# Attention in a graph and transformer kernel: the fp32 product of probabilities and values replaced by three one-pass products

## The reference

```python
h = _layernorm(x, ln1_g, ln1_b)
q = (h @ wq + bq).reshape(B, S, N_HEADS, dk)      # the first block has no biases
k = (h @ wk + bk).reshape(B, S, N_HEADS, dk)
v = (h @ wv + bv).reshape(B, S, N_HEADS, dk)
scores = jnp.einsum('bqhd,bkhd->bhqk', q, k) / np.sqrt(dk).astype(np.float32)
attn = jax.nn.softmax(scores, axis=-1)
ctx = jnp.einsum('bhqk,bkhd->bqhd', attn, v).reshape(B, S, D)
x = x + ctx @ wo + bo
h2 = _layernorm(x, ln2_g, ln2_b)
moe_out = _moe(h2.reshape(-1, D), router_w, router_b, w1, b1, w2, b2)
return x + moe_out.reshape(B, S, D)
```

## Time and profile before

| what | value |
|---|---|
| time, median of 3 | 3896.92 us |
| profiled execution: its own time | 3900.6 us |
| its span | 3898.9 us |
| mean granted TensorE clock | 0.861 of full speed |
| TensorE matmul busy | 2943.6 us (75%) |
| VectorE busy | 1631.0 us (42%) |
| ScalarE busy | 808.3 us (21%) |
| GpSimd busy | 187.3 us (5%) |
| line 804, values product, x960 records | 376.9 us busy |
| line 955, maxima, x480 | 269.8 us busy |
| line 893, exponentials, x480 | 230.9 us busy |

### The profile page before, as it was taken

The page is one execution under the profiler, slowest core; times in us unless marked ns, Lnnn a source line. Parts: engine busy times, 40 slices in busy tenths (PEclk is TensorE's granted clock), DMA queues, the critical chain, the costliest instruction groups (busy, mean ns, idle before and its releaser), DMA issues. The chain is left out here.

```text
span 3898.9 us, 41895 instructions
## 1 busy us (share of the span) xinstructions
PE 2943.6 (75%) x12919; PEld 1988.3 (51%) x12920; DVE 1631.0 (42%) x3241; ACT 808.3 (21%) x1669; POOL 187.3 (5%) x215
## 2 busy tenths in 40 slices
PE   5888739976999972998578589965865688898735
PEld 3555516555666641665264266653643556665523
DVE  6777651134566532343523601030132346565323
ACT  1222310103444410111201211110111124443100
POOL 0000000000000003111100000001010000000033
PEclk9999869998999975998788799967977899999767
DMA  6000270200000005996420300005322000000054
GB/s 244 2 0 0 49 220 13 51 22 9 6 6 3 0 3 151 307 312 198 115 108 2 80 6 11 1 1 166 122 70 51 25 11 4 5 3 0 1 171 131
DMA packets 123973, 261.27 MB, mean 67 GB/s; under 512 B 40586, under 2 KB 41818, under 8 KB 122587
## 3 DMA queue, kind: packets, MB, share of 16 engines
q1 hardware_dynamic: 47643, 122.34, 10.3%
q10 hardware_dynamic: 46848, 92.38, 7.3%
q0 software_dynamic: 29376, 45.16, 4.0%
HBM read 185.71 MB, written 74.02 MB: 67 GB/s over the span
## 5 line engine op out<-in xcount | busy, mean ns | idle before, releaser
L804 PE MATMUL ps<-probs,V 125*128 125x500 f32 (+1 forms) x960 | 376.9, 514 | 0.0
L955 DVE TENSOR_REDUCE mx<-ps 125x1 f32<-125x500 f32 (+1 forms) x480 | 269.8, 588 | 170.0 <-PE ps L787 167.4
L893 ACT ACTIVATE probs<-ps 125x500 f32<-125x500 f32 (+1 forms) x480 | 230.9, 517 | 373.8 <-PE ps L796 363.4
L243 PE MATMUL ps<-onehot_src,onehot_dst 125*128 x1200 | 259.5, 356 | 42.3 <-DVE onehot_dst L219 16.1
L218 DVE TENSOR_SCALAR onehot_src<-iota,src_f 125x1250 f16 x400 | 218.2, 545 | 113.4 <-PE ps L243 100.7
L795 PE MATMUL ps<-Q_hi_twice,K_hi_lo 128*125 128x500 f32 (+1 forms) x480 | 208.7, 435 | 61.2 <-DVE Q_hi_twice L937 32.2
L787 PE MATMUL ps<-K_hi_lo,Q_hi_twice 128*125 128x500 f32 (+1 forms) x480 | 219.5, 464 | 16.0 <-DVE mx L955 7.3
L1377 PE MATMUL ps<-w2s,hT 128*78 128x512 f32 (+1 forms) x480 | 218.1, 601 | 3.6 <-ACT hT L1402 3.6
L804 PEld LDWEIGHTS ps<-probs,V 125*128 125x128 f32 x960 | 164.0, 192 | 105.9 <-issue 105.0
L1442 DVE COPY yb<-ps 78x512 f32<-78x512 f32 (+1 forms) x100 | 68.8, 688 | 348.4 <-PE ps L1377 270.3
L243 PEld LDWEIGHTS ps<-onehot_src,onehot_dst 125*128 x1200 | 121.7, 102 | 173.7 <-issue 118.7
(11 more groups left out here) (341 smaller groups left out, 4681.8 us busy)
## 6 DMA issues: line engine op xcount, KB each, us to landing
room<-in_L_ffn_w_p ACTq DMA_DIRECT2D x72, 512.0 KB, 5.6
w2s<-in_L_ffn_w ACTq DMA_DIRECT2D x72, 512.0 KB, 6.6
buf<-zeros SPq DMA_DIRECT2D x37, 512.0 KB
slabs<-ah_spill SPq DMA_DIRECT2D x20, 585.9 KB
xb<-buf SPq DMA_DIRECT2D x64, 156.0 KB
yb<-yb POOLq DMA_DIRECT2D x64, 156.0 KB, 6.6
xb<-buf SPq DMA_DIRECT2D x36, 250.0 KB
tv<-in_L_ffn_tv_W_p SPq DMA_DIRECT2D x2, 4096.0 KB
```

The source lines that it names most:

```text
L243: mm_ = pe.matmul(ps[:, 3 * half + c, 0:cn], ohd[:, slot, :].rearrange("p o n -> p (o n)"), ohs[:, slot, c0:c0 + cn].rearrange("p o n -> p ...
L804: mm = pe.matmul(ps[:, ACC + n, 0:cn], V[:, t, :], PT[:, t % 2, c0:c0 + cn], start=(t == 0), stop=(t == T - 1))
L893: act.activation(PT[:, t % 2, c0:c0 + cn], ps[0:P, ST + n, 0:cn], ACT.Exp, scale=SCALE).then_inc(p_out, 1)
L955: v.tensor_reduce(mx[:, t, n:n + 1], ps[0:P, SQ + cc % 2, 0:cn], AX.X, ALU.max)\
```

## The change

- The probabilities exist in two f32r halves. ScalarE writes each exponential twice, to PH (rounded to f32r) and to PT (fp32). GpSimd makes PL = PT - PH in one instruction of 125x1250 per tile.
- V is split into VH and VL the same way, once per head on VectorE.
- The values product is now VH PH + VL PH (times_v) and, two tiles later, VH PL (rest_times_v), behind a semaphore p_lo of GpSimd. lo_done counts it and frees the PL slot and, for the last tile, the context.
- minus_max uses f32r operands with an identity of 126 columns, and its third row lies in bank ST+2. The projection's third chunk and minus_max(0) wait accordingly.
- Tile 0 of a head waits chunk by chunk for the projection's copies and the row, no longer for all.
- PT, wo and bo now lie in the memory of x (`spare`). x is written to DRAM (x_spill) in the first norm block of the transformer and read back in the norm block behind attention.
- The constant tri is freed after the start.

```diff
+        VH, VL = pair("V", [P, T, 128])
+        PT = spare(P, (2, N))
+        PH, PL = pair("probs", [P, 2, N])
+        eye = sb("eye_r", [P, P + 1], f32r)
...
-        ROW = [ps[DH:DH + 1, SQ, 0:500], ps[DH:DH + 1, SQ + 1, 0:500], ps[0:1, SQ, 0:250]]
+        ROW = (SQ, SQ + 1, ST + 2)
...
                 def times_v(h, t, n):
                     c0, cn = CH[n]
-                    if n == 0:
-                        pe.wait_ge(p_out, h * 30 + (3 * t + 3))
-                    mm = pe.matmul(ps[:, ACC + n, 0:cn], V[:, t, :], PT[:, t % 2, c0:c0 + cn],
-                                   start=(t == 0), stop=(t == T - 1))
+                    pe.wait_ge(p_hi, h * 30 + (3 * t + n + 1))
+                    pe.matmul(ps[:, ACC + n, 0:cn], VH[:, t, :], PH[:, t % 2, c0:c0 + cn], start=(t == 0), stop=False)
+                    mm = pe.matmul(ps[:, ACC + n, 0:cn], VL[:, t, :], PH[:, t % 2, c0:c0 + cn], start=False,
+                                   stop=False)
...
+                def rest_times_v(h, t):
+                    pe.wait_ge(p_lo, h * T + (t + 3))
+                    for n, (c0, cn) in enumerate(CH):
+                        mm = pe.matmul(ps[:, ACC + n, 0:cn], VH[:, t, :], PL[:, t % 2, c0:c0 + cn], start=False,
+                                       stop=(t == T - 1))
+                    mm.then_inc(lo_done, 1)
...
-                            mm = pe.matmul(ROW[n][:, P * t - c0:P * t - c0 + P], negm[:, t:t + 1],
-                                           k.ident[0:P, 0:P], start=True, stop=True)
+                            o = (P + 1) * (t - c0 // P)
+                            mm = pe.matmul(ps[0:1, ROW[n], o:o + P + 1], negm[:, t:t + 1],
+                                           eye[:, :], start=True, stop=True, skip_group_check=True)
...
                 def tiles(h, j, those, has_next, has_second):
                     for t in those:
-                        if t == 0:
-                            ready = h * 9 + 18 if has_next else H * 9
-                            pe.wait_ge(qk_hi, ready)
-                            pe.wait_ge(qk_lo, ready)
-                            pe.wait_ge(row_hi, h * 3 + 3)
                         for n in range(3):
+                            if t == 0:
+                                ready = h * 9 + (12 + 3 * n) if has_next else H * 9
+                                pe.wait_ge(qk_hi, ready)
+                                pe.wait_ge(qk_lo, ready)
+                                pe.wait_ge(row_hi, h * 3 + (n + 1))
...
+                        if t >= 2:
+                            rest_times_v(h, t - 2)
 
                 def between(h, j, chunk, has_next, has_second):
                     for n in range(3):
                         times_v(h, T - 1, n)
+                    rest_times_v(h, T - 2)
                     if has_next:
+                        pe.wait_ge(p_out, h * 30 + 30)
                         minus_max(h + 1)
+                    rest_times_v(h, T - 1)
                     if has_second:
-                        project(h + 2)
+                        project(h + 2, row=h * 3 + 6)
...
+                pe.wait_ge(qk_hi, 18)
+                pe.wait_ge(qk_lo, 18)
                 minus_max(0)
...
                         act.wait_ge(pv_done, h * T + (max(t - 1, 0) + 1))
+                        act.wait_ge(p_lo, h * T + (t + 1))
                         for n, (c0, cn) in enumerate(CH):
                             act.wait_ge(st_done, h * 30 + (3 * t + n + 1))
+                            act.activation(PH[:, t % 2, c0:c0 + cn], ps[0:P, ST + n, 0:cn], ACT.Exp,
+                                           scale=SCALE).then_inc(p_hi, 1)
                             act.activation(PT[:, t % 2, c0:c0 + cn], ps[0:P, ST + n, 0:cn], ACT.Exp,
                                            scale=SCALE).then_inc(p_out, 1)
...
+            @block.gpsimd
+            def _(pool):
+                pool.sem_inc(p_lo, 2)
+
+                def remainder(h, t):
+                    pool.wait_ge(p_out, h * 30 + (3 * t + 3))
+                    pool.wait_ge(lo_done, h * T + (t + 1))
+                    pool.tensor_tensor(PL[:, t % 2, :], PT[:, t % 2, :], PH[:, t % 2, :].bitcast(fp32), ALU.subtract)\
+                        .then_inc(p_lo, 1)
...
-                    v.tensor_copy(V[:, :, 0:DH], Vall[:, :, bass.ds(h * DH, DH)]).then_inc(v_in, 1)
+                    v.tensor_copy(VH[:, :, 0:DH], Vall[:, :, bass.ds(h * DH, DH)]).then_inc(v_in, 1)
+                    v.wait_ge(v_in, h * 2 + 1)
+                    v.tensor_tensor(VL[:, :, 0:DH], Vall[:, :, bass.ds(h * DH, DH)], VH[:, :, 0:DH].bitcast(fp32),
+                                    ALU.subtract).then_inc(v_in, 1)
...
-        norm_rows(nc, k, x, res, have_stats=True, beside=[(g1[:, :], a[pre + "ln1_g_c"]), (b1[:, :], a[pre + "ln1_b_c"]),
+        norm_rows(nc, k, x, res, have_stats=True, beside=in_two(rowtiles(x_spill), x) + [(g1[:, :], a[pre + "ln1_g_c"]), (b1[:, :], a[pre + "ln1_b_c"]),
...
-            wo, bo, biased = sb(c2, "wo", [128, C, D]), sb(c2, "bo", [P, D]), sb(c2, "biased", [P, 2, D])
+            spare = Room(x128)
+            wo, bo, biased = spare(128, (C, D)), spare(P, (1, D))[:, 0, :], sb(c2, "biased", [P, 2, D])
...
-                  beside=[(b2r[:, :], a[pre + "b2"]), (wr[:, :, :], kchunks(a[pre + ("router_w" if bias else "wr")]))]
+                  beside=in_two(x, rowtiles(x_spill)) + [(b2r[:, :], a[pre + "b2"]), (wr[:, :, :], kchunks(a[pre + ("router_w" if bias else "wr")]))]
```

More of the change, by code:

```diff
@@ L767, in _, with project @@
                 pe.sem_inc(pv_done, 1)
-                pe.wait_ge(ones_set, 2)
-                def project(h, between=lambda: None):
+                pe.sem_inc(lo_done, 2)
+                pe.wait_ge(ones_set, 5)
+                def project(h, between=lambda: None, row=None):
                     pe.wait_ge(w_split, h + 2)
                     for n, (c0, cn) in enumerate(CH):
+                        if row is not None and ST + n == ROW[2]:
+                            pe.wait_ge(row_hi, row)
                         o = ps[:, ST + n, 0:cn]
@@ L912, in _ @@
                 schedule(act, tiles, between)
+            @block.gpsimd
[6 more added lines that the diff above has]
+                        .then_inc(p_lo, 1)
+                with pool.Fori(0, H) as h:
+                    for t in range(T):
+                        remainder(h, t)
             @block.vector
@@ L919, in _ @@
                 v.memset(K2[DH:DH + 1, :, :].bitcast(fp32), 1.0).then_inc(ones_set, 1)
-                v.memset(V[:, :, DH:128], 1.0).then_inc(ones_set, 1)
+                v.memset(negm[:, :].bitcast(fp32), 0.0).then_inc(ones_set, 1)
+                v.memset(VH[:, :, DH:128].bitcast(fp32), 1.0).then_inc(ones_set, 1)
+                v.memset(VL[:, :, DH:128].bitcast(fp32), 0.0).then_inc(ones_set, 1)
+                v.tensor_copy(eye[:, :], k.ident[0:P, 0:P + 1]).then_inc(ones_set, 1)
                 def rest(out, psum, hi, b):
@@ L1982, in program @@
         k.ones = ctx.enter_context(nc.sbuf_tensor("ones", [128, 128], fp32))
-        k.tri = ctx.enter_context(nc.sbuf_tensor("tri", [128, 128], fp32))
         k.ones16 = ctx.enter_context(nc.sbuf_tensor("ones16", [128, 128], bf16))
@@ L1986, in program @@
         k.c_sel, k.c_win = a["c_sel"], a["c_win"]
-        x = ctx.enter_context(nc.sbuf_tensor("x", [P, T, D], fp32))
+        x128 = ctx.enter_context(nc.sbuf_tensor("x", [128, T, D], fp32))
+        x = x128[0:P]
         start_done = ctx.enter_context(k.semaphore(nc, "start_done"))
@@ L1997, in program, with _ @@
         yb0, yb3 = scratch("yb0", (NB0, D)), scratch("yb3", (NB3, D))
+        x_spill = scratch("x_spill", (N, D))
         scr1, scr2 = scratch("scr_minmax", (2, ET)), scratch("scr_tab", (NW, 4), i32)
-        load(nc, k, [(k.ident[:, :], a["c_ident"]), (k.tri[:, :], a["c_tri"])])
-        with nc.Block() as block:
-            @block.vector
-            def _(v):
-                v.memset(k.ones[:, :], 1.0)
-                v.memset(k.ones16[:, :], 1.0)
-                v.tensor_copy(k.tri16[:, :], k.tri[:, :])
-        with ExitStack() as c2:
+        with ExitStack() as c2:
+            k.tri = c2.enter_context(nc.sbuf_tensor("tri", [128, 128], fp32))
+            load(nc, k, [(k.ident[:, :], a["c_ident"]), (k.tri[:, :], a["c_tri"])])
+            with nc.Block() as block:
+                @block.vector
+                def _(v):
+                    v.memset(k.ones[:, :], 1.0)
+                    v.memset(k.ones16[:, :], 1.0)
+                    v.tensor_copy(k.tri16[:, :], k.tri[:, :])
             zeros = c2.enter_context(nc.sbuf_tensor("zeros", [128, 2 * D], fp32))
```

30 lines of the change are left out of this document (16 added, 14 removed).

## The result

The changed kernel takes 3986.97 us (median of 4, 3978.89 to 3993.08) against 3896.97 before: ratio 1.0232, interval 1.0206 to 1.0257. It is slower by 90 us. The forecast was 3928 and its range ended at 3968: the sign was right, the size was not.

A forecast was written before the change was run, and what follows sets the result against it. TensorE was taken to bound tiles 5 to 9, VectorE tiles 0 to 4 as much. Twelve heads +14, heads 0 and 7 -5, spill +22 made +31, 3928 us on the median's scale; 8-in-10 range 3853 to 3968.

The forecast's parts named there:

- One-pass price: Values product in each tile: three one-pass products take 1.72 us instead of 2.1, saving TensorE 0.38 us a tile.
- VectorE bounds tiles 0 to 4: First half of a head: VectorE's 3.81 us a tile do not shrink, so TensorE's 0.38 us gain is given away.
- The meeting: Tiles 0 to 4: GpSimd's reads block VectorE's two-input product, 4.45 us a tile (chance 0.52), or do not (0.27).
- A longer wait is cut by the loop itself: Tiles 0 to 4: a 0.8 us wait closes the loop at 4.45 us; most longer waits give the same period.
- E_1 to E_5: From tile 1's held score product to tile 5's: four tiles each 0.64 us longer, +2.6 us a head.
- Split_lo: Tile 5: VectorE's low half of the weights comes behind a subtraction; the maxima behind it hold TensorE, +1.3 us.
- Tiles 5 to 9: Second half of a head: TensorE stays the bound and gains 0.38 us on four tiles, -1.5 us.
- Start of a head: Tile 0 waits chunk by chunk for the projection's copies: -1.0 us with VectorE's product blocked, -1.6 without.
- End: End of a head: cheaper minus_max, but the projection waits for GpSimd's last subtraction; 5.0 to 5.1 us against 5.3, -0.2.
- Heads 0 and 7: First and last head of each attention: +0.2 and -2.6 us, both stages together -5 us.
- Spill: Write and reload of x in the norm blocks, covered by nothing: 11 us a stage, 22 in all, bounds 10 and 32.
- the free case: Tiles 0 to 4: GpSimd and VectorE do not meet; -3.4 us a head, -41 in twelve, 3873 us; chance 0.27.

The follow-up runs named there:

- e11: Changed kernel with spill unawaited, low products earlier, subtraction in thirds but then left out, and VectorE's reciprocal left out too: 3806.96 us, ratio 0.9756.
- e12: Kernel before the change with VectorE's reciprocal of the normalisation left out: 3878.71 us, ratio 0.9935.
- e1: Changed kernel with GpSimd subtracting only 2 columns and filling the rest of the low half by memsets, so it only writes: 3887.93 us, ratio 0.9969.
- e2: Changed kernel with the low products of two tiles back issued ahead of the values products: 3936.82 us, ratio 1.0090.
- e3: Kernel before the change with only the write of x to DRAM and its reload added: 3940.38 us, ratio 1.0108.
- e4: Changed kernel with GpSimd's subtraction left out whole, the low half zero, all products kept: 3886.44 us, ratio 0.9953.
- e7: Kernel before the change with only tile 0's wait for the projection's copies made chunk by chunk: 3882.11 us, ratio 0.9952.
- e9: Changed kernel with spill unawaited, low products ahead of values products, and GpSimd's subtraction in five instructions of 250 columns: 3865.31 us, ratio 0.9910.

## Why the prediction was wrong

- **One-pass price**: right, 0.38 us a tile (e11, e12; tiles 5 to 9 at 3.45). **VectorE bounds tiles 0 to 4**: right.
- **GpSimd's subtraction**: 2.8 taken, 2.88 measured.
- **The meeting**: the right case of the two, and shown by e1. Its price failed at the step "ScalarE's first exponential ... GpSimd starts at 6.1": I let GpSimd wait for the exponentials alone, in a loop of two tiles and 4.45 us. It also waits for the slot of PL, which the low products free, which stand behind the held score product, which waits for the maxima, which stand behind the blocked product. That loop spans one tile and takes 5.5 us. The change has the slot's wait (lo_done), and I did not follow it. e2 shows it: with the low products ahead of that wait GpSimd starts behind the exponentials and tiles take 4.1 us. "A longer wait is cut by the loop itself" held there only. E_1 to E_5 was 1049.63 to 1070.75, 21.1 us against 15.3, +5.8 for +2.6; in the mean of the twelve heads +6.1.
- **The clock in the loop**: put at nothing. The prediction has a lower clock only at a head's start; with the longer idle of the loop it came into the tiles too (0.71 to 0.74 in one tile of ten heads, above; 1.00 there in e1), some 8 us of the twelve heads' loss.
- **Split_lo**: +1.3 taken. In this head it was not blocked (1071.54, before GpSimd's 1072.49), in head 0 it was. Mean 1.00 us against 0.68. The term was too high in the twelve heads, where the late subtraction let it pass.
- **Tiles 5 to 9**: E_5 to E_9 went from 15.1 to 13.9 us, -1.2 for -1.5; the step from E_5 to E_6 was 3.6 us before as well.
- **Start of a head**: -1.8 here for -1.0, -1.7 and -1.5 in the means. The first tile, from E_0 to E_1, takes 4.8 us at the lower clock and not the 6.9 of the prediction. **End**: -0.5 for -0.2, from 5.8 to 5.2 us in each of the twelve; E_9 stood at 1064.87, half a microsecond ahead of where I had counted from. TensorE waits 0.70 us for GpSimd before the projection, as described.
- So the twelve heads give +2.5 and +3.1 each, +33 for +14.
- **Heads 0 and 7**: -5 forecast, +16.5 measured (the +49.9 less the twelve heads). Head 0, from its copy of V to the next, is 6.5 and 6.1 us longer, where +0.2 stood (its own terms, -3.4 +1.8 +2.0, make +0.4). The start was right: the first transposed score stands 4.1 us later from the block's start, for +3.8. But the nine tiles give nothing: in the fence below, the weights' low half is blocked to 3.35 us (maxima 6.15 apart across it, not 3.44), and the first two tiles take 8.8 us instead of 7.3: the granted clock over them is 0.52 of 2.4 GHz, near the lower level (last fence line), where the kernel before had 0.77 in its own two. Head 7, with its normalisation of head 6, meets GpSimd too, which I had costed only in the twelve. VectorE of the kernel after, head 0 (maxima of tiles 0, 2, 5 and 6), and the busy time of the first two tiles, columns as in the earlier trace rows:

```profile
991.72 0.68 DVE L1001 TENSOR_REDUCE mx<-ps 125x1 f32<-125x500 f32 x1 [3.06 <-PE ps L792]
...
1000.49 1.90 DVE L1001 TENSOR_REDUCE mx<-ps 125x1 f32<-125x500 f32 x3 [1.93 <-PE ps L792]
...
1010.81 1.91 DVE L1001 TENSOR_REDUCE mx<-ps 125x1 f32<-125x500 f32 x3 [1.54 <-PE ps L792]
1013.69 3.35 DVE L987 TENSOR_TENSOR w_lo<-room,w_hi 128x512 fp32r<-128x512 f32 x1 [0.97 <-ACT w_hi L887]
1016.96 1.58 DVE L1001 TENSOR_REDUCE mx<-ps 125x1 f32<-125x500 f32 x3
...
991.70:1000.40 8.70, 8.48 (x25) 6.82 (x25) 3.50 (x6) 6.17 (x14) 4.99 (x2) 0.52 0.00 0
```

- **Spill**: 22 forecast, 33.2 by the traces, 42 by e3 (interval 35 to 50). A store of these rows took no less than the load of them: the block was 17.6 us, beside the 17.1 of my rows, so the first blocks stood at the upper end of "+5 to +11" (+11.1, +10.4). The reload was +6.7 and +5.0 where I had "0 to +5". 11 a stage was too little, and the upper bound of 32 too low.
- The differences to the forecast: +19 from the twelve heads, +21 from heads 0 and 7, +11 from the spill, +9 that no step spoke of. The 10 us in the routers and experts are not explained.

So the case was chosen right, without a row that decided it, and three terms were too small: the loop, heads 0 and 7, and the spill. Against the free case the parts fit: e3 to e4, the products and all without meetings, is -54 us (forecast -41 - 5 = -46), of which e7's edit gives 19; the meetings, with the wait at a head's end, add 100 where my two cases were 55 apart.

The Trainium skill, page "SBUF — State Buffer", section "Who interferes with whom", says that a VectorE instruction with two SBUF inputs contends with a GpSimd instruction that reads SBUF and not with one that only writes; e1 and the kernel after agree (0.41 and 1.68 us). It says too that the other "fully blocks" until the instruction ends; the product ended 0.27 us after GpSimd's, which agrees; in e9 the weights' low half waited for more than one instruction.

## What to carry to other kernels

When an engine is brought in that can block another, draw its start from every semaphore it waits on, the freeing of its buffer too, and follow that back: if the chain passes the blocked instruction, the loop is one tile long and the wait is paid whole. Put what frees the buffer ahead of what waits for the blocked engine, and cut the blocking instruction into pieces, but leave gaps between them (e9). Look at the granted clock where the loop makes TensorE idle. Gain on an engine shows only where no other has the same period, and a transfer in a short block costs its whole length unless its wait is moved to where the memory is next used.

## What was not expected of the hardware

- A small VectorE instruction with one SBUF input waited as well: `negm`, 125x10, tensor_scalar, 2.66 us beside GpSimd's subtraction against 0.17 without (e2). The reciprocal, also with one input, never did (1.71 or 1.72 us in every kernel that has it).
- Three GpSimd instructions for one cost 0.29 us more (3.17 against 2.88) in tiles where VectorE has no product with two SBUF inputs, and 0.45 (3.33) where it has one.
- VectorE's instruction with two SBUF inputs could wait for a whole row of GpSimd instructions: 7.16 us for 0.68 in e9.
- 2.56 MB from SBUF to DRAM in rows of 2 KB held a block for 17.6 us, some 145 GB/s, where the earlier trace rows show 272 in a stretch of graph spills.
